# A soft mixture of experts: its combine fed from stored logits, with tokens on partitions

## The reference, cut to what matters

```python
logits = (einsum('tzd,ed->tze', x, phi_w) + phi_b).reshape(t, z, 64, 32)   # 4096 tokens x 2048 slots
D = softmax(logits, axis=3)                     # dispatch: over the 32 slots of an expert
C = softmax(logits, axis=2)                     # combine: over the 64 experts, for each slot number
X_tilde = einsum('tznp,tzd->npd', D, x)         # then clip, layer norm, tanh
Y_tilde = einsum('npd,ndH->npH', X_tilde, expert_w) + expert_b[:, None, :]
Y = einsum('tznp,npH->tzH', C, Y_tilde)         # added to x with weight 0.5
```

## Time and profile before

| | us |
|---|---|
| median of 3 runs | 2159.27 (2156.85 to 2159.78) |
| span of the profiled execution | 2183.6 |
| PE busy in it | 1858.0 (85%) |
| DVE busy | 1647.8 (75%) |
| POOL busy | 1232.5 (56%) |
| ACT busy | 1193.9 (55%) |
| DMA, mean rate | 75 GB/s |

### The profile page before, as it was taken

The page is one execution under the profiler, slowest core; times in us unless marked ns, Lnnn a source line. Parts: engine busy times, 40 slices in busy tenths (PEclk is TensorE's granted clock), DMA queues, the critical chain, the costliest instruction groups (busy, mean ns, idle before and its releaser), DMA issues.

```text
span 2183.6 us, 24397 instructions
## 1 busy us (share of the span) xinstructions
PE 1858.0 (85%) x6162; PEld 924.7 (42%) x6180; DVE 1647.8 (75%) x2142; ACT 1193.9 (55%) x2869; POOL 1232.5 (56%) x796
## 2 busy tenths in 40 slices
PE   4089886788888851997999989999997999999999
PEld 3067732333333441776333344444443433344445
DVE  5223488999999960334999968888987999958887
ACT  2322286555555424222999964433566999953342
POOL 3735407999999755452899930000796999910000
PEclk9999998999999965998999999999998999999999
DMA  8123393455555312332400000000651300000000
GB/s 272 48 82 98 114 158 98 173 173 173 174 173 176 113 38 71 91 90 92 96 0 0 0 1 0 1 0 0 183 154 40 77 0 0 0 1 5 7 9 20
DMA packets 102452, 163.85 MB, mean 75 GB/s; under 512 B 10897, under 2 KB 65972, under 8 KB 102242
## 3 DMA queue, kind: packets, MB, share of 16 engines
q1 hardware_dynamic: 94178, 146.59, 22.6%
q0 software_dynamic: 8192, 16.30, 2.3%
HBM read 125.27 MB, written 38.14 MB: 75 GB/s over the span
## 4 chain that ended last, share of the span: by engine, by line
PE 36%; DVE 32%; issue 15%; POOL 10%; ACT 4%; DMA 1%; another core or an unknown queue 1%; DVEq 1%; POOLq 0%; SPq 0%; PEldq 0%; ACTq 0%; PEld 0%
PE ps L2217 10%; DVE arena L1583 6%; PE ps L1941 5%; PE ps L1928 5%; DVE arena L1589 5%; DVE arena L1581 5%; DVE arena L1645 4%; POOL slot_inputs L567 3%; PE ps L2075 3%; DVE arena L1522 2%; PE ps L2247 2%; POOL arena L616 2%; POOL arena L641 2%; DVE c_phiT L1522 1%; PE ps L2219 1%
## 5 line engine op out<-in xcount | busy, mean ns | idle before, releaser
L2163 PE MATMUL ps<-arena 128*128 128x512 f32 x512 | 251.8, 615 | 14.0 <-POOL arena L641 13.8
L649 POOL TENSOR_TENSOR arena<-arena 128x864 f32<-128x864 f32 x128 | 210.3, 1643 | 74.2 <-DVE arena L1581 71.8
L2154 PE MATMUL ps<-c_phiT,arena 128*128 128x512 f32 x512 | 243.4, 599 | 5.6 <-DVE arena L1583 5.1
L2217 PE MATMUL ps<-XT,c_phiT 128*128 (+1 forms) x512 | 243.3, 593 | 4.9 <-DVE arena L1621 3.9
L641 POOL TENSOR_TENSOR arena<-arena 128x1024 f32<-128x1024 f32 x128 | 246.7, 1929 | 0.0
L579 POOL DMA_INDIRECT token_outputs<-arena x128 | 124.6, 973 | 151.3 <-DVE arena L1412 112.9
L2247 PE MATMUL ps<-arena 128*128 128x512 f32 x480 | 208.6, 592 | 0.0
L681 POOL TENSOR_TENSOR arena<-arena 128x1024 f32<-128x1024 f32 x24 | 48.0, 2008 | 268.0 <-DVE arena L1752 265.8
L950 ACT ACTIVATE arena<-arena 128x32 f32<-128x32 f32 x640 | 195.7, 311 | 0.0
L1522 DVE TENSOR_TENSOR_SCAN arena<-ps,arena 128x1024 f32<-128x1024 f32 x84 | 187.9, 2274 | 6.0 <-POOL arena L611 5.9
L2075 PE MATMUL ps<-arena,c_ident 128*128 128x512 f32 x336 | 161.0, 601 | 25.5 <-POOL arena L616 25.5
(11 more groups left out here) (266 smaller groups left out, 3771.5 us busy)
## 6 DMA issues: line engine op xcount, KB each, us to landing
arena<-input_gates SPq DMA_DIRECT2D x128, 512.0 KB, 3.7
arena<-value_rows SPq DMA_DIRECT2D x32, 512.0 KB, 5.3
arena<-slot_inputs SPq DMA_DIRECT2D x32, 258.0 KB
arena<-in_L_ffn_w SPq DMA_DIRECT2D x32, 256.0 KB
arena<-token_outputs SPq DMA_DIRECT2D x16, 512.0 KB, 7.8
slot_inputs<-arena SPq DMA_DIRECT2D x1, 4128.0 KB, 13.4
slot_inputs<-zero SPq DMA_DIRECT2D x1, 4128.0 KB, 32.9
token_outputs<-arena SPq DMA_DIRECT2D x1, 4096.0 KB
```

Source lines behind the costliest of these rows:

```text
L649: pool.tensor_tensor(Ed[:, r, PSLOT * NA:].rearrange("p (n q) -> p n q", q=PSLOT), Lc[:, r, PSLOT * NA:].rearrange("p (n q) -> p n q", q=P ...
L2154: ins = pe.matmul(pbank(2 * h + c), xts[:, r // 2, :], phiT[:, at:at + CHUNK], start=True, stop=True)
L2163: ins = pe.matmul(pbank(4 + 2 * h + c), xns[:, r // 2, :], Dd[:, r, CHUNK * c:CHUNK * (c + 1)], start=start, stop=stop, skip_group_check=True)
L2217: ins = pe.matmul(pbank(t % 4), phiT[:, P * t:P * (t + 1)], xt(b, c), start=True, stop=without_m)
```

## The change

The dispatch's logits are stored in DRAM as the combine's input, and the combine works by tiles of 128 tokens. SP stores every unit of `Lc` (0.5 MB) in `lrows`, and `copy_L` waits for the store of four units before. After the last store SP loads one tile (128 x 2048, 1 MB) at a time into a ring of four buffers `Lt`. POOL takes the maxima off with one instruction. PE turns the tile in 16 transposes (`turn_logits`), ACT exponentiates it from PSUM in two instructions, DVE adds the 16 blocks with one `tensor_reduce` whose input view has the block index innermost (a step of 128 words), PE's `total` and ACT's two instructions are now over 128 columns, and DVE weighs. `combine` has the exponentials as PE's weights and `Yt` as the moving matrix, so that its output has tokens on partitions and goes into x without a turn. `mCT`, the bf16 parts, `logits_T`, `less_m`, `tree`'s five steps, `copy_y`, `turn_y` and the halved last chunk go away. The loops start at FIRST = 3 and PE combines LAG = 3 tiles behind; the ring of `Ec` has four tiles.

```diff
+FIRST = 3
+LAG = 3
+LAST_TOKENS = ((TILES - 4, TILES - 2), (TILES - 2, TILES - 1), (TILES - 1, TILES))
...
+        Lt = [Lt[1], XN_flat[:, 0:SOFT], XN_flat[:, half_rows:half_rows + SOFT], Lt[0]]
+        part = [b2[:, j, :] for j in range(2)]
...
             # SyncE, after the loads of We and eb
+                for u in range(UNITS):
+                    sp_.wait_ge(sem("Lc"), UNITS * s + u + 1)
+                    sp_.dma_start(lrows[P * (u // 2):P * (u // 2 + 1), HW * (u % 2):HW * (u % 2 + 1)], Lc[:, u % RING, :])\
+                        .then_inc(sem(f"got{u % RING}"), 16)
+                for t in range(TILES):
+                    q = t % len(Lt)
+                    for u in (2 * t, 2 * t + 1):
+                        sp_.wait_ge(sem(f"got{u % RING}"), stored_rows(s, u))
+                    if t >= len(Lt):
+                        sp_.wait_ge(sem("LT"), 2 * (TILES * s + t - len(Lt) + 1))
...
+                    sp_.dma_start(Lt[q], lrows[P * t:P * (t + 1), :]).then_inc(sem(f"row_in{q}"), 16)
...
             # GpSimd, after the dispatch
+                pool.wait_ge(sem("mx"), s + 1)
+                for t in range(TILES):
+                    rows = Lt[t % len(Lt)].rearrange("p (n q) -> p n q", q=PSLOT)
+                    pool.wait_ge(sem(f"row_in{t % len(Lt)}"), loaded_rows(s, t))
+                    pool.tensor_tensor(rows, rows, mxC[0][:, t, :].unsqueeze(1).to_broadcast([P, NEXP, PSLOT]), ALU.subtract)\
+                        .then_inc(sem("Lm"), 1)
...
             # ScalarE, in copy_L
+                        hold(act, sem(f"got{r}"), stored_rows(s, 0) - 16 + 16 // RING * (u - r))
...
+                def exp_T(t, p):
...
+                    act.activation(Ec[t % RING][:, 8 * p:8 * (p + 1), :].rearrange("p a b -> p (a b)"), pbank(2 * p, 2), ACT.Exp)\
+                        .then_inc(sem("Ec"), 1)
...
+                for t in range(FIRST, TILES):
+                    inverse_sum(t - 2)
+                    exp_T(t, 0)
+                    exp_T(t, 1)
...
             # VectorE
+                def tree(t):
...
+                    dve.tensor_reduce(part[t % 2], Ec[t % RING].rearrange("p a b -> p b a"), AX, ALU.add).then_inc(sem("tree"), 1)
...
+                def weigh(t):
+                    dve.wait_ge(sem("Rz"), first + t + 1)
+                    dve.tensor_tensor(Ec[t % RING], Ec[t % RING], Rz[t % len(Rz)].unsqueeze(1).to_broadcast([P, ST, P]), ALU.mult)\
+                        .then_inc(sem("C"), 1)
...
+                tree(0)
+                slot_scale(0)
+                slot_scale(1)
+                tree(1)
+                weigh(0)
...
+                tree(2)
+                for t in range(FIRST, TILES):
+                    weigh(t - 2)
+                    c, step = (t - PER_CHUNK - LAG) // PER_CHUNK, (t - PER_CHUNK - LAG) % PER_CHUNK
+                    if c >= 0 and step == 0:
+                        add_and_measure(c)
+                    if s == 0 and c >= 0 and step == 1:
+                        ln_apply(4, c, c % 2)
+                    tree(t)
+                weigh(TILES - 2)
...
             # TensorE
+                def turn_logits(t):
...
+                    pe.wait_ge(sem("Lm"), v + 1)
...
+                        for j in range(8):
+                            at = 8 * p + j
+                            ins = pe.transpose(pbank(2 * p + j // 4)[:, P * (j % 4):P * (j % 4 + 1)],
+                                               Lt[t % len(Lt)][:, P * at:P * (at + 1)], ident[:, :])
...
+                def combine(t):
...
+                    pe.wait_ge(sem("C"), v + 1)
+                    for j in range(ST):
+                        ins = pe.matmul(token_bank(s, t)[:, P * at:P * (at + 1)], Ec[t % RING][:, j, :], Yt[:, j, :],
+                                        start=(j == 0), stop=(j == ST - 1))
...
+                for t in range(FIRST, TILES):
+                    turn_logits(t)
+                    combine(t - LAG)
+                    total(t - 1)
...
+                total(TILES - 1)
                 if s:
+                    for t in range(TILES - LAG, TILES):
+                        combine(t)
                     return
+                values(0)
+                low_rank(0)
+                combine(TILES - 3)
+                project_kq(0, 0)
+                project_fg(0, 0)
+                combine(TILES - 2)
```

More of the change, by code:

```diff
@@ L57 @@
 SP = 4
-BY_PE = (7, 4)
 NB = 4
@@ L963, in soft, with slot_square @@
                 copy_xn(TILES - 1, 1)
[L965 to L970, removed]
+                first = TILES * s
+                def slot_square(h):
+                    act.wait_ge(sem("slot_c"), 2 * s + h + 1)
                     act.activation(slotB[:, 1024 * h:1024 * (h + 1)], slotA[:, 1024 * h:1024 * (h + 1)], ACT.Square)\
@@ new lines, in soft @@
+                weigh(TILES - 2)
+                if s == 0:
+                    ln_apply(4, CHUNKS - 2, 0)
+                weigh(TILES - 1)
+                if s:
+                    for t0, t1 in LAST_TOKENS:
+                        residual(t0, t1)
+                    return
+                silu_kq(0, 0)
+                scan(0)
+                scan(1)
+                add_and_measure(CHUNKS - 1)
+                scan(2)
+                ln_apply(4, CHUNKS - 1, 1)
+                scan(3)
@@ new lines, in total @@
+                def total(t):
+                    v = first + t
+                    pe.wait_ge(sem("tree"), v + 1)
+                    if v:
+                        pe.wait_ge(sem("Rz"), v)
+                    if t == 0:
+                        pe.wait_ge(sem("slot_r"), 2 * s + 1)
+                    if t == 1:
+                        pe.wait_ge(sem("Yt"), 4 * s + 1)
+                    pe.matmul(pbank(4)[:, 0:P], same_p[:, :], part[t % 2], start=True, stop=True).then_inc(sem("total"), 1)
@@ L2233, in slot_outputs @@
                         ins.then_inc(sem("Yt_ps"), 1)
-                def total(v):
-                    pe.wait_ge(sem("tree"), 5 * (v + 1))
-                    pe.matmul(pbank(4), same_p[:, :], t1, start=True, stop=True).then_inc(sem("bank4"), 1)
-                def combine(v, c, early, beside={}):
-                    if not early:
-                        pe.wait_ge(sem("yT"), v)
-                    for t in range(ST):
-                        if t in beside:
-                            beside[t]()
-                        if t % 8 == 0:
-                            pe.wait_ge(sem("C"), 2 * v + t // 8 + 1)
-                        ins = pe.matmul(pbank(5), Yt[:, t, :], Ec[c][:, t, :], start=(t == 0), stop=(t == ST - 1))
-                    ins.then_inc(sem("yT_ps"), 1)
@@ L2250, in turn_y @@
-                def turn_y(v, early):
-                    pe.wait_ge(sem("yT"), v + 1)
-                    if not early:
-                        pe.wait_ge(sem("s_add"), v)
-                    for j in range(PER_CHUNK):
-                        ins = pe.transpose(pbank(6)[:, P * j:P * (j + 1)], yT[:, P * j:P * (j + 1)], ident[:, :])
-                    ins.then_inc(sem("y_tok"), 1)
-                def total_half(v, h):
-                    pe.wait_ge(sem("tree"), 5 * (v + h + 1))
-                    pe.matmul(pbank((4, 7)[h])[:, half(h)], same_p[:, :], t1[:, half(h)], start=True, stop=True).then_inc(sem("bank4"), 1)
```

499 lines of the change are left out of this document (162 added, 337 removed).

## The result

The changed kernel takes 2176.52 us (median of 4 runs, 2175.01 to 2179.27) beside 2159.43 for the kernel before: 17 us slower, ratio 1.0085 with a 95% interval of 1.0070 to 1.0099. The forecast was 2139: it missed by 37.5 us and had the sign wrong. The time lies inside the stated range.

The account below looks back on a forecast made before the run. It took all four engines as full in the dispatch and PE alone in the combine. Combines -42 (s = 1) and -9.5 (s = 0), stalls +28, clock +3 gave -20.5 off 2159.3: 2139 us, range about 2102 to 2185.

Parts of the forecast that it names:

- The stalls of the dispatches: Dispatches: first store stands behind the `We` and `eb` loads, so ACT's fifth copy is late by 8.5 and 20 us.
- the clock: Dispatch of s = 1: PE's logits run at half clock after idling, +3 us (0 to 5).
- The mechanism of the combine: Combine: POOL's subtraction and DVE's weighing exclude each other at a shared port, 6.05 us a tile, above PE's 5.8.
- the strided sum: Combine: DVE's reduce at a step of 128 words takes 3.5 us, between ends of 2.2 and 4.5.
- I take 3.8, the middle: Combine: POOL's subtraction of 2048 columns, between 3.64 and 3.93 us by slopes of other instructions.
- the port's sum: Combine: POOL's 3.8 plus the weighing's 2.25 one after the other, 6.05 us a tile; 6.1 taken for s = 1.
- The start: Head of each combine: join, subtraction, turn, slots' normalisation and waits for POOL; `tree(2)` ends 38 us after 1911.97 in s = 1.
- DVE's own work in s = 1: Combine of s = 1: DVE's sum and weighing together take 5.75 us a tile.
- The tail of s = 1: End of the last combine: `total` 0.35, three combines on PE 11.2, residual 0.6, together 12.2 us.
- The allowance of 0.48 us a tile for scalings that wait: Combine of s = 0: four scalings may wait for POOL once a chunk, 0.95 us more a tile; middle taken, 7.3.
- C: Rival: DVE waits for POOL 1.9 us a tile instead of 0.3, giving 2232; break-even 0.35 more a tile; chance 0.25.
- B: Rival: strided sum costs nothing extra (2.2 us) and scalings never meet POOL, giving 2110; chance 0.15.

Follow-up runs that it names:

- e1_spread: Changed kernel with the loads of `We` and `eb` in twelve pieces between the stores of units 4 to 26; 2143.37 us, ratio 0.9923 to the kernel before.
- e4_rzps: Changed kernel with the inverse sums of tiles 2 to 28 in s = 1 in PSUM, so `weigh` has one SBUF input; 2164.37 us, ratio 1.0020.
- e9_keepadds: Changed kernel with loads spread, s = 1 inverse sums in PSUM, and DVE's sum as four contiguous additions, POOL still subtracting; 2272.89 us, ratio 1.0420.
- e3_nosub: Changed kernel without POOL's subtraction of the maxima in the combine; 2115.37 us, ratio 0.9792 to the kernel before.
- e14_sub54: Changed kernel with POOL's subtraction on 54 of 64 groups, 1728 of 2048 columns; 2147.46 us, ratio 0.9943 to the kernel before.
- e10_sub27: Changed kernel with POOL's subtraction cut to 27 groups, 864 of 2048 columns; 2126.62 us, ratio 0.9845 to the kernel before.
- e13_quarters: Changed kernel with POOL's subtraction in four instructions of 512 columns, nothing left out; ratio 1.0086 to the kernel before.
- e11_halves: Changed kernel with POOL's subtraction in two instructions of 1024 columns, nothing left out; ratio 1.0106 to the kernel before.
- e2_contig: Changed kernel with DVE's sum reading its 2048 columns contiguously, so it adds the wrong elements; 2160.01 us, ratio 1.0006 to the kernel before.
- e7_sub2d: Changed kernel with POOL subtracting a plain contiguous tile instead of the repeated maxima; ratio 1.0078 to the kernel before.

## Why the prediction was wrong

**What held.** The stalls of the dispatches: +31.8 in the stages against a forecast of +31.5, and e1_spread gives 33 back by moving the loads alone. That the sums agree so well is in part luck: the second stall was 22.9 us and not 20, its stage grew by 21.8, and no 3 us of the clock show beside it. After PE's pause of 19.0 us one group of four logit products ran at a granted clock of 0.50 to 0.55 (1.2 GHz), 3.57 us at 1708.44 where it takes 1.88 at 2.4 GHz, 1.7 more; from 1712 on the clock is 1.00. The mechanism of the combine held too: the port between POOL and DVE (e4_rzps and e9_keepadds in opposite directions, e3_nosub as its removal), PE no longer full, the strided sum at means of 3.72 and 3.75 us (forecast 3.5).

**The step that failed** is "I take 3.8, the middle" for POOL's subtraction. It takes 4.5, and it enters at four places: the port's sum of both stages, the start of both. In s = 1 the port's sum was 6.05; a turn in which `weigh` waits for POOL takes 6.55, 21 of 32 do, and T is 6.60. In s = 0, `weigh` waited 1.14 us a tile instead of 0.3. The start was 41.4 us to `tree(2)` instead of 38: the two `slot_scale` took 9.91 us, against 6.53 in e14_sub54 and 2.34 without POOL, since with 4.5 us the second meets another of POOL's instructions. So 0.7 us on POOL cost 4 us there.

e14_sub54 puts 3.8 us in: T in s = 1 is 6.12 for a forecast of 6.1, the start 37.4 for 38, and 29 of the 37.5 us are gone. The 6.12 is luck in part. Of 32 weighings two wait, and the tile is DVE's own 5.96, which the prediction had at 5.75, with little on top; with POOL at 2.0 us (e10_sub27) it is still 6.00.

Both ends of my price, 3.64 and 3.93, were below the truth, since both were slopes of other instructions. The subtraction takes 1.26, 2.34 and 4.50 us for 512, 1024 and 2048 columns (e13_quarters, e11_halves, the changed kernel), 2.1 ns a column. And the trace of before had this price. POOL's products L616 (L625 after) are one instruction, which reads the two halves of `Cs` by turns; here two with the first and the second half:

```profile
383.68 2.35 POOL L616 TENSOR_TENSOR arena<-arena,XT 128x1024 f32<-128x1024 f32 x1
...
389.90 2.00 POOL L616 TENSOR_TENSOR c_phiT<-c_phiT,XT 128x1024 f32<-128x1024 f32 x1
```

They alternate without an exception, 2.35 to 2.42 and 2.00 to 2.06 us. L602 is also two groups, of 1.09 to 1.11 and of 1.26 to 1.30 us, and the 1087 of the earlier trace rows is the cheap one. With the dear ones, 1.27 and 2.35, the slope is 2.1 and 2048 columns come to 4.5; with 1.09 and 2.00 it is 1.78 and they come to 3.8, my forecast. Two ends that close together were not bounds.

**Smaller terms.** DVE's own work in s = 1 was 5.96, not 5.75: the sum 0.12 more, the weighing 0.05 less, and the residual addition, 0.15 a tile, I had counted in s = 0 only. It hides behind the port until the port is treated; then it is the bound (e4_rzps). The tail of s = 1, from the end of `tree(31)`, took 13.8 us against 12.2, that of s = 0 11.2 against 9.3. The allowance of 0.48 us a tile for scalings that wait was too large in the changed kernel (0) and a little too small in e14_sub54, 17.7 us over 29 tiles, 0.61. `weigh` waited 0.46 a tile there instead of 0.3, so T was 7.57 against 7.3: 8 of the 8.5 us by which that kernel missed 2139.

**The rivals.** C had the sign and named the mechanism, waits of `weigh` of 1.9 us a tile; they were 0.58 in s = 1 (90.5 us for 32, over 2.25 each) and 1.1 in s = 0. Its break-even, 0.35 us a tile more in both stages, is what decided: T came out 0.5 and 0.4 above the forecast. B fell: even with a sum of 2.27 us (e2_contig) the kernel stays at 2160, and the scalings do meet POOL.

**Open.** What makes two of POOL's instructions of one form cost 2.00 and 2.35 us. A plain operand, shorter instructions and another operation left the subtraction as it was, and writing over an input is not it (L700, which does, 2.00 us; L694, which doesn't, 2.00). What fits is where the operands lie. By the kernel's own offsets, if its tensors start at multiples of four words, the dear pairs are those whose second operand starts 0 or 3 words past a multiple of four from the first (`Cs` at word 2055 of `XT`, `sp_ln` at 3 and 3084), the cheap ones 1 or 2 (`Cs` at 3082, `sp_ln` at 1030 and 2057, `q_s` and `k_s`, moved by `ODD = 2`). The subtraction's pair is at 0, also in e7_sub2d. No run moved an operand, so this is inferred, and the next kernel to try has the maxima two words further on.

## What to carry over

When an instruction is priced by the slope of others, look at every single duration of those lines and not at a group's mean or median, which can hide two prices; the bounds are the slopes of every row of that engine, not two that lie near each other; and a term that enters the sum of a shared port, the start and each wait is the first to vary when the range is worked out. Where two engines share a port, count for each the instructions that need it, the short ones above all: work taken from one side can come back as waiting (e2_contig in s = 0, e9_keepadds), and an operand in PSUM takes an instruction out of the count. A store that releases a ring buffer goes ahead of bulk loads in its queue's order, and the loads in pieces behind.

## What the runs showed of the hardware

- A DVE instruction of two SBUF inputs, or a scaling from SBUF to SBUF, that meets one of POOL's waits for its end, whatever its own length: 0.29 us became 4.46, 0.33 became 4.5, 2.25 became 6.09. A reduce (means of 3.69 us without POOL, 3.72 to 3.82 beside it) and `weigh` with a PSUM input (2.33 beside 2.28) don't wait.
- Cutting POOL's work into shorter instructions didn't shorten the tile: T in s = 1 was 6.60, 6.62 and 6.84 us for one, two and four.
- A DVE reduce that reads SBUF at a step of 128 words takes 3.7 to 3.8 us for 2048 columns, contiguous 2.27. By the Trainium skill, Vector Engine (DVE) Microarchitecture Reference, Measured stream behaviour on trn2, a source that hops 4 KiB at every element costs 1.73 ns a column, 3.54 us for 2048 as an estimate. The step here is 512 bytes and the operation another; the trace's means, 3.69 to 3.82, are 4 to 8% above it. The 2.50 ns that the prediction takes from the same table stand there for both sources, or the destination, at a step of 24 words, and no run here has such a step.
- POOL's `tensor_tensor` of two full float32 streams has two prices: 1.09 or 1.27 us for 512 columns (L602), 2.00 or 2.35 for 1024 (L616), and 4.50 for the subtraction of 2048.
- SP's queue was held 15.9 us by the four loads of `eb` behind the one of `We`, and what stood behind them waited 8.5 and 22.9 us. The same bytes in twelve pieces between stores held up nothing.
